# The router's comparison cut in two pieces and its position products moved two units back, in a vision tower with a mixture of experts

## The reference

```python
xt = x.reshape(b * s, d)                                   # 592 x 256, after a layer norm
probs = jax.nn.softmax(xt @ router_w + router_b, axis=-1)  # 8 experts
rw, ids = jax.lax.top_k(probs, TOPK)                       # TOPK = 2
rw = rw / (jnp.sum(rw, axis=-1, keepdims=True) + 1e-20)
y = jnp.zeros_like(xt)
for e in range(E):
    w_e = jnp.sum(jnp.where(ids == e, rw, 0.0), axis=-1)
    y = y + w_e[:, None] * _ffn(xt, gate_w[e], up_w[e], down_w[e])
y = y + _ffn(xt, sh_gate_w, sh_up_w, sh_down_w)            # the shared expert
# _ffn(x, g, u, d) = (silu(x @ g) * (x @ u)) @ d, hidden width F = 688
```

## Time and profile before

| | |
|---|---|
| median of 3 runs | 362.44 us (361.62 to 363.1) |
| the profiled execution's own time | 361.26 us |
| its span, first to last instruction | 359.5 us |
| PE, DVE, ACT, POOL busy | 92%, 63%, 48%, 38% of the span |
| mean granted clock of PE | 0.967 |

### The profile page before, as it was taken

The page is one execution under the profiler, slowest core; times in us unless marked ns, Lnnn a source line. Parts: engine busy times, 40 slices in busy tenths (PEclk is TensorE's granted clock), DMA queues, the critical chain, the costliest instruction groups (busy, mean ns, idle before and its releaser), DMA issues.

```text
span 359.5 us, 8376 instructions
## 1 busy us (share of the span) xinstructions
PE 330.2 (92%) x3508; PEld 276.9 (77%) x3508; DVE 226.1 (63%) x577; ACT 172.7 (48%) x370; POOL 134.8 (38%) x75
## 2 busy tenths in 40 slices
PE   8999989979599887999989999998979989898996
PEld 5785578757399786999989999998536777677864
DVE  1299879996766262454655555455784688665784
ACT  0205863455232133577666667733216782386700
POOL 5201059100705803487667777775520000000010
PEclk9999999996769997899999999999999999999999
DMA  8990005200221332158637657229100000000002
GB/s 277 415 372 5 2 2 167 91 0 3 88 73 62 101 121 79 27 183 257 235 116 235 216 182 230 91 66 290 55 0 2 2 2 5 0 1 2 5 2 67
DMA packets 16016, 37.09 MB, mean 103 GB/s; under 512 B 1930, under 2 KB 9729, under 8 KB 15976
## 3 DMA queue, kind: packets, MB, share of 16 engines
q1 hardware_dynamic: 14576, 33.68, 27.8%
q0 software_dynamic: 960, 2.43, 2.1%
q10 hardware_dynamic: 440, 0.41, 0.4%
HBM read 30.76 MB, written 5.75 MB: 102 GB/s over the span
## 4 chain that ended last, share of the span: by engine, by line
PE 47%; DVE 27%; ACT 12%; issue 7%; DMA 4%; POOL 1%; another core or an unknown queue 1%; POOLq 0%; ACTq 0%; DVEq 0%
PE ps L1528 6%; PE ps L1530 6%; PE ps L1529 6%; PE ps L1727 5%; DVE ps L1029 3%; PE ps L1823 3%; PE ps L1737 3%; ACT w0h L540 2%; ACT w1h L540 2%; PE ps L1799 2%; DMA yrowhi<-yg_d,of_hi 2%; PE ps L1336 2%; ACT gact L564 2%; DVE stage_l L839 2%; DVE mx L833 2%
## 5 line engine op out<-in xcount | busy, mean ns | idle before, releaser
L1029 DVE TENSOR_TENSOR ps<-gact,ps 128x256 f32<-128x256 f32 (+3 forms) x60 | 26.2, 437 | 44.2 <-ACT gact L564 41.5
L1250 POOL TENSOR_TENSOR w0l<-raw,w0h 128x1536 fp32r<-128x1536 f32 (+1 forms) x12 | 39.9, 3322 | 30.0 <-ACT w0h L540 30.0
L1262 POOL TENSOR_TENSOR rstd<-vtmp,cst 128x3 f32<-128x3 f32 (+1 forms) x8 | 6.7, 839 | 116.8 <-DVE vtmp L738 64.7
L1250 POOL TENSOR_TENSOR w1l<-raw,w1h 128x1536 fp32r<-128x1536 f32 (+1 forms) x12 | 39.8, 3314 | 10.3 <-ACT w1h L540 9.7
L564 ACT ACTIVATE gact<-ps 128x256 f32<-128x256 f32 (+3 forms) x60 | 23.3, 388 | 29.9 <-PE ps L1530 19.3
L568 ACT ACTIVATE hrh<-ps 128x256 fp32r<-128x256 f32 (+1 forms) x48 | 18.4, 384 | 30.6 <-DVE ps L1029 30.1
L1034 DVE TENSOR_TENSOR hrl<-ps,hrh 128x256 fp32r<-128x256 f32 (+1 forms) x48 | 20.3, 423 | 18.4 <-ACT hrh L568 17.6
L1324 PE MATMUL ps<-cst 128*128 128x512 f32 x62 | 28.9, 611 | 0.0
L1528 PE MATMUL ps<-xg0h,w1h 128*128 128x256 f32 x88 | 26.4, 300 | 0.0
L1528 PE MATMUL ps<-xg1h,w0h 128*128 128x256 f32 x88 | 25.6, 291 | 0.0
L1529 PE MATMUL ps<-xg0l,w1h 128*128 128x256 f32 x88 | 25.6, 290 | 0.0
(11 more groups left out here) (300 smaller groups left out, 952.7 us busy)
## 6 DMA issues: line engine op xcount, KB each, us to landing
raw<-in_wexp SPq DMA_DIRECT2D x18, 768.0 KB, 4.2
raw<-in_wexp SPq DMA_DIRECT2D x9, 640.0 KB, 4.2
xg_d<-zero SPq DMA_DIRECT2D x8, 256.0 KB, 10.3
xgs<-xg_d SPq DMA_DIRECT2D x8, 256.0 KB, 4.4
stage_l<-in_xT SPq DMA_DIRECT2D x6, 320.0 KB, 4.7
yg_d<-y SPq DMA_DIRECT2D x7, 256.0 KB, 3.3
stage_l<-in_tokW SPq DMA_DIRECT2D x6, 128.0 KB, 5.3
wq_l<-in_wql SPq DMA_DIRECT2D x1, 640.0 KB
```

The lines of the kernel that those rows point to most:

```text
L1029: V.tensor_tensor(up, gact[i % 2][rows_of(c), 0:n], up, ALU.mult).then_inc(S("hm"), 1)
L1250: nc.gpsimd.tensor_tensor(wset[x % 2][1][w], raw[w], wset[x % 2][0][w].bitcast(F32), ALU.subtract).then_inc(S("w_lo"), 1)
```

## The change

The comparison becomes two functions. `compare_first` (copies, equality, greater-than) stands behind unit 0 on DVE, `compare_last` (the rest) behind unit 1, with a semaphore `compared` between them. `destinations` moves from behind unit 1 to behind unit 3, `router_probs` from behind unit 3 to behind unit 4. On PE the position products with their wait for `sel` move from behind unit 1's gate and up products to behind unit 3's, and the wait for `lg_shift` there goes away. `turn(0)` is written earlier in the loop body, but is still run behind unit 10.

```diff
-            def router_compare():
+            def compare_first():
                 dve.wait_ge(S("lg_shift"), 1)
                 for t in range(TT):
                     other = lg[:, t, :].unsqueeze(1).to_broadcast([P, E, E])
                     V.tensor_copy(gt[:, t], other).then_inc(S("gt"), 1)
                 dve.wait_ge(S("gt"), TT)
                 link(V.tensor_tensor(eq2, gt2, mine, ALU.is_equal))
-                link(V.tensor_tensor(gt2, gt2, mine, ALU.is_gt))
+                V.tensor_tensor(gt2, gt2, mine, ALU.is_gt).then_inc(S("compared"), 1)
+
+            def compare_last():
+                dve.wait_ge(S("compared"), 1)
                 link(V.tensor_tensor(eq3, eq3, lt.rearrange("p e f -> p (e f)").unsqueeze(1).to_broadcast(
                     [P, TT, E * E]), ALU.mult))
                 link(V.tensor_tensor(gt3, gt3, eq3, ALU.add))
...
-            router_compare()
-            steps = {1: destinations, 3: router_probs, 5: overflow, 6: sources, 8: weights_of_each}
+            steps = {0: compare_first, 1: compare_last, 3: destinations, 4: router_probs, 5: overflow,
+                     6: sources, 8: weights_of_each}
             for u in range(NH):
                 shared(u, u // 2, u % 2)
...
                 shared_gate_up(u, u // 2, u % 2)
-                if u == 1:
+                if u == NH - 2:
+                    turn(0)
+                if u == 3:
 
                     pe.wait_ge(S("sel"), 1)
...
                     last.then_inc(S("pos_mm"), 1)
-                if u == NH - 2:
-                    turn(0)
-                if u == 3:
-                    pe.wait_ge(S("lg_shift"), 1)
                 if u % 2 == 1 and u >= 3:
                     shared_down(u - 3, u // 2 - 1)
```

## The result

Measured against the kernel before in turns, the changed kernel took 366.16 us in the median of 5 runs (365.0 to 367.11), the kernel before 362.66 us (361.62 to 363.3). The ratio is 1.0133, with a 95% interval of 1.0089 to 1.0176: **slower by 1.3%**. Forecast was 363.9 us, at most 365.3. The medians differ by 3.5 us; 1.3% of 362.66 is 4.8. The profiled execution took 365.96 us with a span of 364.2 us, against 361.26 and 359.5 before: 4.7 us more. (Ratios are taken from undisturbed runs alone, so they are not always the quotient of two medians.)

A forecast was written before the change was run, and what follows sets the result against it. TensorE, busy 92% of the span, was taken as the bound: only its pauses count. New pauses add 1.7 us, 0.2 is taken back, so 362.44 + 1.5 = 363.9 us, range 361.2 to 365.3.

The forecast's parts named there:

- Steps 1 and 2: TensorE pauses 0.3 us before unit 2, then 1.1 to 1.4 before unit 3, behind the comparison's first piece.
- Step 3: Behind unit 3: the comparison's second piece ends at 111.15, so position products start with no further pause, or 0.1 us.
- Step 4: Sum at the first down projection: it starts at 113.3 instead of 111.56, 1.7 us later.
- Step 5: Destinations, scatters and row loads move about 5.2 us; rows keep 5.7 us before the transposes; costed at nothing, up to 1.
- rival (e): At the transposes: gathered rows land late and TensorE waits; +2.5 us, 364.9 us, chance 0.05.
- Step 6: Probabilities move behind unit 4; at unit 7 0.2 of the 1.7 us is taken back, leaving 1.5.
- the seventh: Behind unit 7: ScalarE's 4.43 us idle time moves with the units, 1.5 us stay; if at a fixed moment, 1.2 absorbed.
- rival (d): Units 3 to 4: the two new pauses, close together, lower the clock; +4.6 us, 367.0 us, chance 0.08.
- (a): Before units 8 and 9: ScalarE's idle time stays at its moment; +0.3 us, 362.7 us, chance 0.20.
- (b): Around unit 1: TensorE returns to 2.4 GHz later than 104.5; +0.5 us, 362.9 us, chance 0.10.
- (c): Last shared down projection: the shifted 2.41 us pause no longer lowers the clock; -1.6 us, 360.8 us, chance 0.12.

The follow-up runs named there:

- the third chip: Kernel before unaltered 0.9956; changed kernel unaltered 1.0129; before with low weights early plus two fillers 0.9965, or plus scatters held to the fifth unit 0.998.
- the probes: Kernel before with 24 copies on ScalarE ahead of unit 6's Silu, and kernel before with five scatters instead of ten; no time given for the last chip.

## Why the prediction was wrong, point by point

Steps 1 and 2 were right: a small pause before unit 2, and one before unit 3 from the comparison's first piece. The row of the latter shows 0.95 us of idle time (in four further profiles 0.82 to 0.98), where 1.1 to 1.4 stood; but by the starts, 109.46 - 106.57 = 2.89 us against 1.69 for a unit, it cost 1.2 us, as forecast. Step 3 held (first product without a pause). Step 4: 1.57 us at the first down projection, 1.7 forecast. Step 5, as to its rows: right, the transposes at 137.45 waited for nothing, so rival (e) didn't come about there; by then TensorE was 4.19 us late itself. But the 5.7 us of cover that I counted lay partly in ScalarE's idle time: on chips without it the rows were late, by 0.17 us in the changed kernel and by 1.34 to 3.24 in the three variants with late scatters. Step 6: the 0.17 us before unit 7 was there again, so nothing of the lag was taken back; 1.66 us were left, 1.5 forecast.

**The step that failed is the seventh**, together with the price put on the fifth. There I left two cases for ScalarE's idle time: that it moves with the units, or that it stays at a fixed moment. "Nothing else of the trace sits at that moment" was the argument against the second, and it was wrong: ten scatters ran on GpSimd from 109.93, and the idle time ended at 124.31, 1.9 us behind the end of the last one (121.54 + 0.91). It moves with them. Step 5 moved them by 5.2 us (5.4 measured, 0.26 of it from in front of the stage) and costed that at nothing, having asked only who waits for the rows. TensorE moved by only 1.9 us, so it reached the wait for the struck unit 12.5 us behind the first scatter instead of 15.8, while that wait ended at 16.2 and 16.4: a pause of 3.71 us took the place of those of 1.11, 0.56 and 0.67. Measured: 0.77 us more at unit 9, and then 1.5 us behind it, over which the clock was at 0.61 and 0.88. That the pause lowered the clock is read from the windows of this kernel, here and on the third chip; no run took the pause away alone.

The clock: rival (d) had the right mechanism with the wrong trigger. Its sum, +4.6 us, came close to the 4.7 of the profile by luck: it rested on pauses of 0.3 and 1.3 us which in fact left the clock at 1.00; the pause of 3.71 us wasn't in the list. Rivals (a), (b) and (c) didn't come about: the idle time was not at a fixed moment; TensorE was at 0.50 until 104.5 as before, and over 104.50 to 106.00 at 0.84 against 0.95; and behind the pause of 2.40 the clock was at 0.54, as at 0.56 before.

What of it is general to the kernel and what to the chip: in the two comparisons of the pair in which the idle time is there, 1.0133 and 1.0129; in the one without it 0.9986. There the kernel before, by its relative with the five fillers, has a VectorE instruction of 3.84 us and a pause of 3.18 us on TensorE, the changed one 1.95 and 1.12. That this difference pays for the new pause before unit 3 fits the sizes, and was not isolated further. Each chip served on one occasion only, and each program was profiled in one execution there, so whether the chip or the occasion decides on the idle time is not separated.

Open stays what the idle time is. In the one execution of each, ScalarE did not stand still throughout, and five scatters did not suffice. Whether the signal of TensorE comes late, or instructions do, the probes don't tell; the short idle times on both engines would go with either. The queues that the page names "instruction" show no packet between 6 and 14.7 us behind the first scatter in six of the seven profiles that have the idle time; in the seventh, that with held scatters on the third chip, there is one between 11 and 12 us. As far as these queues are recorded, that speaks against an instruction fetch that lands late. The last 0.5 us of the 4.7 was not traced either.

## What to carry to other kernels

When an edit moves a burst of DMAs, ask not only who waits for its data, but which unexplained idle times lie inside it: measure them from the burst's first instruction, not from the span's start, and work out how far the waiting engine will have got when they end, if they move with the burst and it doesn't. Where small VectorE instructions with two SBUF operands run beside a GpSimd instruction of 3.5 us, every reordering decides anew which of them is caught; to put the GpSimd work where VectorE has none of them was worth more than any shift of VectorE's steps on the chips without ScalarE's idle time (0.9904 and 0.9889, and 0.9806 with the pause before the last down projection filled; on the chip with it, this last kernel had 0.9965). And repeat a difference of 1% on another chip before calling it the kernel's.

## What the runs showed that I had not expected

Around a burst of ten indirect scatters ScalarE's Silus are held up until 14.3 to 14.7 us behind its first instruction in seven profiles (the two of the first comparison, four on the third group's chip and one on the last), and until 8.6 to 8.7 us in all of these but the one with held scatters. On three other chips no profile shows it. TensorE has its own pause in the same place: its row with 1.11 us in the earlier trace rows stands at 123.46 - 109.93 = 13.5 us, and in the kernel with held scatters on the third chip, at 130.00 - 116.28 = 13.7:

```profile
130.00 0.28 PE L1529 MATMUL ps<-w0h,hsh 128*128 128x256 f32 x1 [1.12 <-issue]
```

A VectorE instruction of 0.19 us on 128x40 took 3.85 us beside GpSimd's 3.50, one of 0.18 took 1.95, and `wover<-slot,wts`, 0.29 in the kernel before, 1.25. A filler of 128x512 in f32 costs TensorE 0.88 us (7.03 us for 8). The clock fell behind pauses of 3.71, 3.18 and 2.40 us and stayed at 1.00 behind the 0.95 before unit 3 and the 1.11 of the earlier trace rows. In between it isn't one-valued: behind the last pause, of 1.44 us, of the changed kernel with the low weights moved it was at 0.57 over 138 to 145, behind that of 1.47 us of the kernel with the comparison in one piece at 1.00 over 137 to 144; in the kernel with held scatters a pause of 1.49 us, shortly behind the one of 1.12, goes with a mean of 0.64 over 130 to 137, and in the one with eight fillers a pause of 2.41 us left it at 1.00.
